# Opening of an attention stage reordered, and its last steps paired by half of the matmul array

## The reference

```
x = x + retention(norm(x))     # 4 heads, rope, decaying state over chunks, gated output, + its own residual
x = x + ffn(norm(x))           # token shift, r = sigmoid(xr W_r), k = relu(xk W_k)^2, out = r * (k W_v)
x = x + attention(norm(x))     # 16 heads of 16 channels, 1024 x 1024 scores per head
x = x + ffn(norm(x))           # the same weights again

scores = einsum('bhqd,bhkd->bhqk', q, k) / sqrt(16) + bias[bucket(j - i)]
attn   = softmax(scores); out = einsum('bhqk,bhkd->bhqd', attn, v)
```

## Time and profile before

| | |
|---|---|
| median of 3 runs | 3088.31 us (3087.98 to 3089.7) |
| the profiled execution: its own time | 3088.87 us |
| its span in the trace | 3086.4 us |
| PE busy, share of the span | 2885.0 us, 93% |
| DVE, ACT, POOL | 66%, 56%, 41% |
| row score matmuls (L736) | 2048, 803.4 us busy |
| column score matmuls (L762) | 2048, 789.5 us busy |
| weighing (L785) | 8192, 641.3 us busy |
| maxima on DVE (L1453) | 2048, 1261.7 us busy |
| exponentials on ACT (L1196) | 2048, 1120.5 us busy |

### The profile page before, as it was taken

How to read it: one execution, slowest core, us unless ns; L and a number is a source line. 1 busy time by engine, 2 the same in 40 slices (tenths; PEclk the granted TensorE clock), 3 DMA queues, 4 the chain that set the end, 5 groups by cost and what they waited for, 6 DMA issues and landing times.

```text
span 3086.4 us, 51535 instructions
## 1 busy us (share of the span) xinstructions
PE 2885.0 (93%) x18786; PEld 1495.0 (48%) x18786; DVE 2045.4 (66%) x4319; ACT 1739.7 (56%) x3667; POOL 1250.0 (41%) x1764
## 2 busy tenths in 40 slices
PE   5989999899998999989999999999999899998997
PEld 3643356433664336643466434653346533465334
DVE  4469735796457954589545994469934699346982
ACT  2428834388344873448644586436854368543784
POOL 2325533255332543335443354334543345433453
PEclk8979999999999999999999999999999999999999
DMA  6041000510005000140001400023000320003200
GB/s 176 1 105 20 2 1 1 122 30 2 1 13 124 16 2 1 24 114 16 2 1 41 97 16 1 1 62 76 16 1 1 82 56 16 1 1 82 56 2 14
DMA packets 54779, 107.58 MB, mean 35 GB/s; under 512 B 12400, under 2 KB 34976, under 8 KB 54400
## 3 DMA queue, kind: packets, MB, share of 16 engines
q1 hardware_dynamic: 54528, 104.29, 14.6%
HBM read 56.66 MB, written 36.72 MB: 30 GB/s over the span
## 4 chain that ended last, share of the span: by engine, by line
PE 71%; DVE 13%; SPq 4%; POOL 3%; issue 3%; DMA 3%; ACT 2%; POOLq 0%; DVEq 0%; ACTq 0%
PE psum L736 18%; PE psum L785 16%; PE psum L554 10%; DVE mx L1453 7%; PE psum L762 4%; PE psum L836 4%; SPq L446 3%; PE psum L890 2%; PE psum L817 2%; PE psum L874 2%; DMA parts<-mixed 2%; PE psum L625 2%; PE psum L589 2%; PE psum L893 2%; POOL X L1559 1%
## 5 line engine op out<-in xcount | busy, mean ns | idle before, releaser
L1453 DVE TENSOR_REDUCE mx<-psum 128x1 f32<-128x512 f32 x2048 | 1261.7, 683 | 119.9 <-PE psum L736 119.2
L1196 ACT ACTIVATE Z<-psum 128x512 f32<-128x512 f32 x2048 | 1120.5, 597 | 272.5 <-PE psum L762 240.3
L1649 POOL TENSOR_TENSOR Z<-Z,band_exp 128x256 f32<-128x256 f32 (+1 forms) x1152 | 711.3, 640 | 733.5 <-ACT Z L1196 726.3
L736 PE MATMUL psum<-SK,SQ 63*128 63x512 f32 x2048 | 803.4, 478 | 69.1 <-DVE mx L1453 43.9
L762 PE MATMUL psum<-SQ,SK 64*128 64x512 f32 x2048 | 789.5, 464 | 4.6 <-DMA SQ<-mrow 4.5
L785 PE MATMUL psum<-Z,Vx 128*17 128x256 f32 x8192 | 641.3, 387 | 0.1
L736 PEld LDWEIGHTS psum<-SK,SQ 63*128 63x128 f32 x2048 | 330.6, 192 | 525.0 <-DVE mx L1453 394.2
L554 PE MATMUL psum<-Wqkvg,Z 128*128 128x512 f32 x768 | 368.0, 605 | 1.0 <-ACT Z L1094 1.0
L762 PEld LDWEIGHTS psum<-SQ,SK 64*128 64x128 f32 x2048 | 324.0, 189 | 74.2 <-ACT Z L1196 55.8
L785 PEld LDWEIGHTS psum<-Z,Vx 128*17 128x17 f32 x8192 | 138.4, 95 | 355.1 <-issue 292.0
L1594 POOL TENSOR_TENSOR Z<-Z 128x512 f32<-128x512 f32 x64 | 81.1, 1267 | 304.0 <-DVE Z L1375 304.0
(11 more groups left out here) (121 smaller groups left out, 3269.6 us busy)
## 6 DMA issues: line engine op xcount, KB each, us to landing
parts<-Z SPq DMA_DIRECT2D x32, 512.0 KB
X<-L_attn_a_x SPq DMA_DIRECT2D x8, 1024.0 KB, 5.5
SQ<-parts SPq DMA_DIRECT2D x32, 256.0 KB, 7.5
SK<-parts SPq DMA_DIRECT2D x32, 256.0 KB, 10.6
SQ<-parts SPq DMA_DIRECT2D x16, 512.0 KB, 7.7
SK<-parts SPq DMA_DIRECT2D x16, 512.0 KB, 13.8
out<-X SPq DMA_DIRECT2D x16, 512.0 KB, 19.5
SQ<-mixed SPq DMA_DIRECT2D x96, 64.0 KB, 2.3
```

The lines of the kernel that those rows point to most:

```text
L736: pe.matmul(row_bank(c), SQ[rows_of(h, MAX_ROW), h // 2, i * P:i * P + P], SK[rows_of(h, MAX_ROW), h // 2, 512 * k:512 * k + 512], start=T ...
L1196: nc.scalar.activation(ring[:, n % RING, :], col_bank(n), ACT.Exp)\
L1453: nc.vector.tensor_reduce(mx2[:, blk % 2, col, k:k + 1], row_bank(2 * u + k), AX_X, ALU.max)\
L1649: nc.gpsimd.tensor_tensor(ring[:, n % RING, a:z], ring[:, n % RING, a:z], band_exp[:, 4 * hg + COLS[i], at:at + z - a], ALU.mult)\
```

## The change

- The heads are moved in two pairs: q of heads 0 and 1 (6 DMAs), k of heads 0 and 1 (6), then q and k of heads 2 and 3. The first 8 units use heads 0 and 1 alone, the next 8 heads 2 and 3 (`unit`); a unit waits for its own pair.
- The last projections of v and the first two `mix_k` go into `last_mix_and_rows`, with units between them; the spacing of the later units changes with it, on VectorE too.
- Banks: q and k are projected into banks 3 and 7 instead of 2 and 3, so that the row banks 0 to 2 are free; the first block of maxima is transposed into bank 3 instead of 6. The wait for `kv_r` moves from the first transpose to before the projections and to the first `weigh`.
- `kact` of quarters 2 and 3 lies in `aT`, so `relus` no longer waits for the copies; that wait moves into `tanhs`, since `th` stays where it was.
- In steps 53 to 63 the heads come in the order (1, 0, 3, 2).

The diff, cut to its core (the places that only rename, `QK_BANK`, `max_bank`, `kact_of`, `cols_of` and `spread_pair` in use, are left out):

```
 COLS = (1, 3, 0, 2)
+LAST_COLS = (1, 0, 3, 2)
 RING = 12
...
 oT = cut(7168, 512)
+kact_of = (kact, kact, aT, aT)
 raw = cut(0, 3584).rearrange("p (w c n) -> p w c n", w=7, c=C)
...
-    blk, ii, hh = u // 16, u % 16 // 4, u % 4
+    blk, ii, hh = u // 16, u % 8 // 2, u % 16 // 8 * 2 + u % 2
     return blk // 2 * 4 + hh, blk % 2 * 4 + ii, blk, hh * 4 + ii
...
 K_BANK = (2, 2, 6, 6)
+QK_BANK = (3, 7)
+def cols_of(s):
+    return LAST_COLS if s >= ROWS_END else COLS
...
+def max_bank(blk):
+    return sum_bank(blk) if blk else bank[3]
 def rows_of(h, n=HALF):
...
-    def spread_directly(b, s):
+    def spread_directly(b, pair, s):
...
         stack = (SQ_words, SK_words)[s]
-        for h in range(4):
+        for h in (2 * pair, 2 * pair + 1):
             for group, part in enumerate(((1, 0, 0), (0, 1, 0))[s]):
...
-        for s in range(2):
-            spread_directly(b, s)
+        for pair in range(2):
+            for s in range(2):
+                spread_directly(b, pair, s)
         for h in range(2):
...
         elif q == 2:
-            reach(pe, kv_r, 2 * mix_at(min(b + 1, B - 1), 1) + o + 1)
+            if o == 1 and b < B - 1:
+                need(pe, c_lo, b + 1, 8)
             if b == B - 1:
...
+        v_project(b, 2)
+        if b > 0:
+            mix_k(b - 1, 2, 0)
+        some_rows(1)
+        v_project(b, 3)
+        some_rows(1)
         if b > 0:
+            mix_k(b - 1, 2, 1)
             some_rows(1)
...
             mix_r(b - 1, 2, 1)
-            some_rows(1)
+            some_rows(2)
             ln_transposes(b - 1, 5)
...
             mix_r(b - 1, 3, 1)
-            some_rows(2)
+            some_rows(1)
             mix_kv(b - 1, 3, 0)
-            some_rows(2)
-            mix_kv(b - 1, 3, 1)
-        some_rows(17 - rows + 1)
+        some_rows(16 - rows)
+        if b == 0:
+            some_rows(1)
         max_transpose(b, 0)
+        if b > 0:
+            some_rows(1)
+            mix_kv(b - 1, 3, 1)
         some_rows(AHEAD - rows)
...
-        if u == 0:
-            need(pe, spread_first[0], b, 12)
-            need(pe, spread_first[1], b, 12)
+        if u in (0, 8):
+            need(pe, spread_pair[u // 8][0], b, 6)
+            need(pe, spread_pair[u // 8][1], b, 6)
         for share in (1, 2):
...
             reach(pe, fn_T, 2 * norm_at(b, 3) + 2)
-        elif c == 2:
-            need(pe, c_lo, b, 8)
         elif c > 2:
...
         need(pe, mx_f, b, blk + 1)
-        if blk < 2:
+        if blk == 0:
+            need(pe, c_lo, b, 8)
+        elif blk == 1:
             reach(pe, kv_r, 2 * (mix_at(b - 1, 3) if b > 0 else mix_at(b, 1)) + 2)
...
             need(pe, e_p, b, n - 2)
-        h = 4 * hg + COLS[i]
+        h = 4 * hg + cols_of(s)[i]
         pe.matmul(col_bank(n), SK[rows_of(h), h // 2, j * P:j * P + P],
...
                 need(pe, mx_row, b, s // 8 + 1)
+            if s == 0:
+                reach(pe, kv_r, 2 * (mix_at(b - 1, 3) if b > 0 else mix_at(b, 1)) + 2)
         cols = slice(256 * part, 256 * part + 256)
...
         reach(pe, r_tanh, 2 * mix_at(b, 1) + 2)
+        reach(pe, kv_r, 2 * mix_at(b, 1) + 2)
         for n in range(8):
...
             qk_project(b, n)
-        v_project(b, 2)
-        if b > 0:
-            mix_k(b - 1, 2, 0)
-        v_project(b, 3)
-        if b > 0:
-            mix_k(b - 1, 2, 1)
         last_mix_and_rows(b)
...
         at = mix_at(b, q)
-        if q == 2:
-            need(act, spread_first[0], min(b + 1, B - 1), 12)
-            need(act, first_out[0], min(b + 1, B - 1), 2)
         for o in chunks:
...
             reach(act, p_kv, 2 * at)
-            nc.scalar.activation(kact[:, o, :], bank[K_BANK[q] + o], ACT.Relu).then_inc(k_relu, 1)
+            nc.scalar.activation(kact_of[q][:, o, :], bank[K_BANK[q] + o], ACT.Relu).then_inc(k_relu, 1)
...
         at = mix_at(b, q)
+        if q == 2:
+            for pair in range(2):
+                need(act, spread_pair[pair][0], min(b + 1, B - 1), 6)
+            need(act, first_out[0], min(b + 1, B - 1), 2)
         for pr in range(2):
...
-    def last_mix(b):
-        relus(b, 2)
+    def last_mix(b, begun=False):
+        relus(b, 2, (1,) if begun else (0, 1))
         tanhs(b, 2)
...
             at = (BQ, BK)[s].start + h
-            nc.scalar.activation(split[h][s][:, 0, 512 * g:512 * g + 512], bank[2 + n % 2],
+            nc.scalar.activation(split[h][s][:, 0, 512 * g:512 * g + 512], bank[QK_BANK[n % 2]],
                                  ACT.Identity, bias=vec[:, at:at + 1]).then_inc(c_hi.sem, 1)
         v_copies(2)
+        if b > 0:
+            relus(b - 1, 2, (0,))
         v_copies(3)
...
         if b > 0:
-            last_mix(b - 1)
+            last_mix(b - 1, begun=True)
         max_rows(0)
         for s in range(2):
-            need(act, spread_first[s], b, 12)
+            for pair in range(2):
+                need(act, spread_pair[pair][s], b, 6)
             need(act, first_out[s], b, 2)
...
             if b > 0:
-                if u == 0:
+                if u == 1:
                     ln_norms(b - 1, 5)
-                elif u == 2:
+                elif u == 5:
                     mixes(b - 1, 3, (0,), (0,))
...
                     mixes(b - 1, 3, (0,), (1,))
-                elif u == 3:
+                elif u == 6:
                     gated(b - 1, 2, (1,))
-                elif u == 4:
+                elif u == 8:
                     mixes(b - 1, 3, (1,))
-                elif u == 13:
-                    gated(b - 1, 3, (0,))
                 elif u == 15:
+                    gated(b - 1, 3, (0,))
+                elif u == 16:
                     gated(b - 1, 3, (1,))
```

More of the change, by code:

```diff
@@ L267, in build @@
         parts_out = [tally("sp", f"parts_out_{side}", 2, 16) for side in "qk"]
-        spread_first = [tally("sp", f"spread_first_{side}", 12, 16) for side in "qk"]
+        spread_pair = [[tally("sp", f"spread_pair{pair}_{side}", 6, 16) for side in "qk"] for pair in range(2)]
         spread = [None] + [tally("sp", f"spread{share}", 8, 16) for share in (1, 2)]
@@ L447, in spread_directly @@
                                      split[0][s][HD * h:HD * h + HD, part, :].bitcast(F32))\
-                            .then_inc(spread_first[s].sem, 16)
+                            .then_inc(spread_pair[pair][s].sem, 16)
             def parts_store(b, h, s):
@@ L624, in mix_kv @@
                     for o in range(2):
-                        mm = pe.matmul(bank[6 + pr][:, i * D:i * D + D], kact[:, o, t * P:t * P + P],
+                        mm = pe.matmul(bank[6 + pr][:, i * D:i * D + D], kact_of[q][:, o, t * P:t * P + P],
                                        WT[:, W_V, o, :], start=o == 0, stop=o == 1)
@@ L699, in qk_project @@
                 for c in range(C):
-                    mm = pe.matmul(bank[2 + n % 2], WT[:, A_Q + side, c, h * P:h * P + P],
+                    mm = pe.matmul(bank[QK_BANK[n % 2]], WT[:, A_Q + side, c, h * P:h * P + P],
                                    nT[:, c, 1 + 512 * g:513 + 512 * g], start=c == 0, stop=c == C - 1)
@@ L746, in max_transpose @@
                     need(pe, o_n, b, blk - 1)
-                pe.transpose(sum_bank(blk)[0:16, 0:P], mx[:, blk, :], ident[:, :]).then_inc(mx_tp.sem, 1)
+                pe.transpose(max_bank(blk)[0:16, 0:P], mx[:, blk, :], ident[:, :]).then_inc(mx_tp.sem, 1)
             def score_cols(b, s, i):
@@ L1439, in _ @@
                     tok = slice(512 * g, 512 * g + 512)
-                    nc.vector.scalar_tensor_tensor(split[h][s][:, 1, tok], bank[2 + n % 2], vec[:, at:at + 1],
+                    nc.vector.scalar_tensor_tensor(split[h][s][:, 1, tok], bank[QK_BANK[n % 2]], vec[:, at:at + 1],
                                                    split[h][s][:, 0, tok], ALU.add, ALU.subtract)\
```

12 lines of the change are left out of this document (6 added, 6 removed).

## The result

| | before | after |
|---|---|---|
| median (lowest to highest) | 3089.01 us (3087.98 to 3091.29), 4 runs | 3039.05 us (3036.76 to 3045.01), 4 runs |
| ratio, 95% interval | | 0.984 (0.9824 to 0.9855) |
| the profiled execution: its own time, its span | 3088.87, 3086.4 us | 3038.51, 3035.8 us |

The change takes 50 us off. The forecast was 31 off, to 3057; the range (3034 to 3075) holds the result, the forecast's own 3040 to 3064 just misses it.

What follows compares the result with a forecast made beforehand. PE, busy 93% of the span, was taken as the bound. Opening 20.5 (7 x 3.9 - 6.8), block 0 0.5 and last steps 10 make 31 us off 3088.87, 3057.9; median 0.56 lower, 3057 us; range 3034 to 3075.

Steps and rivals of the forecast that it cites:

- The direction and the mechanism of the opening: Faster at 0.90; in the opening the first unit no longer waits, one gap stays, set by the store of q's parts.
- The transposes 1.0 us earlier: Opening of blocks 1 to 7: relus done before the store lands, so tanhs and then transposes come 1.0 us earlier.
- Three units moved, 2.9 us a block: Behind the opening's transposes 16 units instead of 19: one saves 1.2 us, two 0.85 each, 2.9 together.
- The slow spell, 6.8 us charged: Clock fall behind the gap before the transposes: 1.7 us in all seven blocks, four more than before, 6.8 us lost.
- the single 2.08 us gap: Block 4's idle before the first unit, behind which the clock fell; the remaining gap, longer, was expected to do likewise.
- The last steps, 10 us: Steps 53 to 63: paired column matmuls cut a step from 2.42 us by 0.11, 1.2 a block, 10 us in all.
- rival 2: Last steps run at ScalarE's or PE's own pace, bank wait hidden: 39 us gained there, 3028 us; chance 0.10.
- Block 0, 0.5: Block 0's units start some 6 us earlier, but its first step waits for DMAs of maxima: 0.5 us gained.
- The slower rival: The clock falls in steps 53 to 63, where PE waits: 3.4 us a step, 3155 us; chance 0.05.
- the opening's two terms: Opening of blocks 1 to 7: 1.0 us up to the transposes and 2.9 behind them, 3.9 a block.

Runs made afterwards that it cites:

- Experiment 4: The changed kernel with both relus of quarter 2 waiting for the copies and the store again: 3052.03 us.
- experiment 5: The changed kernel with seven units instead of six ahead of the transposes, VectorE's order shifted to match: 3031.85 us.
- experiment 1: The changed kernel with the old order of heads (1, 3, 0, 2) in steps 53 to 63: 3059.65 us.
- experiment 6: The changed kernel with six banks instead of three for the column matmuls of steps 53 to 59: 3038.42 us.
- experiment 3: The changed kernel with the first unit waiting for all 24 copies and units in the old order of heads: 3075.00 us.
- experiment 7: The changed kernel with the stores of q's parts issued ahead of the six copies of k for heads 2 and 3: 3018.89 us.
- experiment 8: The changed kernel with the edits of experiment 6 and experiment 7 together: 3010.01 us.
- experiment 9: Experiment 8's kernel with the six banks taken up a step and a half later: 3006.97 us.
- experiment 10: Experiment 9's kernel with two units fewer in the opening (AHEAD = 20 instead of 22): 3042.08 us.

## Why the prediction was right, and where it was wrong

**The direction and the mechanism of the opening: right.** The first unit no longer waits, and the store becomes the one wait. Undone singly, both parts tried lose: with the four heads first again 36 us, with the relus waiting again 13. Of these, falls of the clock that the traces show are some 6 of the 13. The pairs alone cost 13 us. So the gain of the opening is not a sum of parts. Earlier units are worth something only where projections are behind them to be reached, and where the wait next in line has moved too.

**The transposes 1.0 us earlier:** measured 0.93 in block 4 and 0.79 in the mean of the seven blocks (5.5 us in all). Experiment 4 took this back.

**Three units moved, 2.9 us a block: measured 3.37.** The part at the end was right: from the last `mix_kv` group to the first column matmul it was 1730.05 - 1721.20 = 8.85 us and is 1702.96 - 1695.30 = 7.66, the 1.2 of VectorE's pace. The two units of the alternating part were taken at 0.85 apiece and gave 2.17 together, 1.09 each. I had chosen near PE's 0.7 because VectorE is busy 2.48 of 4 us there; but from the transposes to the last `mix_kv` group PE also stood idle for VectorE's maxima, 3.3 us before and 2.5 now, and these 0.8 us went with the two units. The seventh unit of experiment 5 took no such idle time with it and gave 0.87, what the prediction had taken.

**The slow spell, 6.8 us charged: wrong, the largest miss in the opening.** Three blocks pay in the trace, as before, and I had charged seven. The step that failed is the size of the gap: PE's work ahead of it ends 15.6 us into the opening (1671.86 - 1.77 - 1654.46), where I had added it up to 14.7, so the gap is 1.8 us and not 2.5. Counted over the openings of all thirteen traces, with the gap directly ahead of the transposes: behind gaps of 2.58 us and more the clock fell 25 times of 25; behind 2.31 and 1.39 it fell, behind 2.17 it didn't; behind 1.62 to 1.91 it fell 11 times of 22 (1 of 5 in the kernel before, 2 of 6 in the changed one, 4 of 6 in experiment 1, 4 of 5 in 6); behind 0.50 to 0.61 2 times of 6; and where there was no gap never, in 35 openings (experiments 3 and 7 to 10). So gaps a little longer than 2.5 us cost in every opening what I charged. At 1.8 the right charge was half the blocks, about what was paid already, and the comparison with the single 2.08 us gap, which I took as a rule, was none. What decides in the cases between stays open.

**The last steps, 10 us: measured 18.** The chain was right, link by link: matmul to exponential 0.58, exponential 0.60, the pair 0.43, the weighing 0.56. The term that was mis-sized is the way back from exponential to PE. I took it from the tanhs' 0.15 at most and settled at 0.13; it is 0.05 here (the exponential ends at 1848.70, the weight load of the fourth matmul starts at 1848.75). So a step is 2.22 and not 2.31. Against 2.42 or 2.43 before that is 0.20 a step where I had 0.11, and eleven steps give 2.2 us where I had 1.2: 1.83 in the nine steps ahead of `w_project` and 0.37 in the two behind it. The bound itself was put right: take the banks away as a limit, and PE's 1.98 appears (experiments 6, 8, 9). This is rival 2, and three banks were what spoke against it, as the prediction said. The Trainium skill, TensorEngine Tiling (Array Packing), section PSUM Bottleneck, says that the copy out of PSUM may become the bottleneck once tiling has made TensorE four times as fast. The traces agree in part: with three banks a step is 2.22 us and ScalarE stands idle once in each, so the wait for a bank bound and not ScalarE's throughput. With six banks ScalarE runs through, at 1.98 us a step, as PE does.

**Block 0, 0.5:** its period is 2.7 us shorter, of which the last steps are 2.2. The 0.5 that is left fits by luck: from its last `v_project` parts to step 53, kernels whose block 0 is the same up to there (the changed one and experiments 1, 4, 5 and 6) take 180.1 to 182.0 us, and the kernel before 180.7. Its units start 7.5 us earlier, and that brought nothing that can be told from this spread.

**The slower rival,** a clock that falls in the last steps: it stayed at 1.00 in 1844:1860, though a step has its wait for the bank.

So 31 became 50: 6.8 more for the spell, 1.9 for the opening's two terms (29.2 - 20.5 - 6.8), 8 for the last steps, and some 3 for the steps before step 53 and the like, which the sum didn't have and no experiment took back. The two large misses point the same way; the range held the result because its lower end had been drawn towards rival 2, not because its terms were right.

## What to carry to other kernels

When a wait is taken away, name the wait that comes next on each engine and ask what it needs itself: here one store stood in a queue behind six copies it had nothing to do with, and moving it past them was worth 20 us more. A part that moves work earlier can lose alone (13 us here) and pay together with the part that gives the freed time something to do, so undo such parts one at a time from the whole instead of judging them alone. And where a saving vanishes or doubles, look at the granted clock in stages that were not edited, before you doubt the mechanism.

## What the runs showed of the hardware that was not expected

- The clock's short fall behind the transposes (mostly 3.4 us at 0.50, 1.3 to 1.7 us lost) is not fixed by the code of the opening: three of seven openings have it in the trace before, all seven in the trace of the kernel that differs in the last steps alone. Whether the edit or the execution decides is not shown. It came behind gaps as short as 0.50 us, and in none of 35 openings where PE had no gap directly ahead of the transposes.
- Two matmuls of 64 rows by 512 columns in different halves of the array, started together, let the next full-height matmul start 0.43 us later; in the same half it is 0.65.
- From the end of an exponential to the weight load that waits for its bank it takes 0.05 us here; from a tanh's end to the transposes it was 0.15.
- Exponentials that follow each other without a wait start 0.47 to 0.52 us apart, 0.50 in the mean of the 20 in experiment 6, though each lasts 0.60.
